# Two layers of cross-attention on one core: values and scores of layer 0 on two 64-row tiles of TensorE

## What is computed

```python
q = x @ Wq + bq;  k = ctx @ Wk + bk;  v = ctx @ Wv + bv
scores = einsum('bkgld,bksd->bkgls', q, k) / sqrt(32) + mask      # 64 keys
out = einsum('bkgls,bksd->bkgld', softmax(scores), v)
x = layer_norm(out @ Wo + bo + x) * gamma + beta
```

## Time and profile before

| what | value |
|---|---|
| median of 3 runs | 1744.62 us (1741.44 to 1746.93) |
| time of the profiled execution | 1741.65 us |
| its span in the profile | 1739.8 us |
| mean granted TensorE clock | 0.999 |
| busy: PE / DVE / POOL / ACT | 98% / 67% / 61% / 33% |

### The profile page before, as it was taken

How to read it: one execution, slowest core, us unless ns; L and a number is a source line. 1 busy time by engine, 2 the same in 40 slices (tenths; PEclk the granted TensorE clock), 3 DMA queues, 4 the chain that set the end, 5 groups by cost and what they waited for, 6 DMA issues and landing times.

```text
span 1739.8 us, 22384 instructions
## 1 busy us (share of the span) xinstructions
PE 1709.9 (98%) x8449; PEld 1426.6 (82%) x8449; DVE 1168.4 (67%) x1106; ACT 581.0 (33%) x669; POOL 1066.3 (61%) x592
## 2 busy tenths in 40 slices
PE   6999999999999999999999999999999999999998
PEld 6888888888888788888888877888888888888887
DVE  7999898888988666565656578446644664466443
ACT  4444354444445433333434223122312231223110
POOL 1777877878788866575756553446734673467331
PEclk9999999999999999999999999999999999999999
DMA  8443244333236577777776856455545654565332
GB/s 239 104 111 86 77 110 108 78 80 78 74 96 165 180 241 228 229 230 224 240 221 223 263 177 194 170 169 182 172 154 170 186 167 155 170 172 180 132 109 97
DMA packets 278127, 280.11 MB, mean 161 GB/s; under 512 B 62330, under 2 KB 230404, under 8 KB 278020
## 3 DMA queue, kind: packets, MB, share of 16 engines
q1 hardware_dynamic: 276672, 276.97, 52.4%
q10 hardware_dynamic: 1348, 1.71, 0.3%
HBM read 175.81 MB, written 102.76 MB: 160 GB/s over the span
## 4 chain that ended last, share of the span: by engine, by line
PE 66%; DVE 13%; POOL 10%; issue 5%; ACT 4%; DMA 2%; SPq 0%; POOLq 0%; DVEq 0%; ACTq 0%
PE ps L53 21%; PE ps L54 21%; PE ps L55 21%; POOL pT0l L1382 3%; POOL pr L1386 2%; DVE small L1106 1%; PE ps L712 1%; PE ps L720 1%; DVE pT1r L1137 1%; DVE pT0r L1137 1%; DVE pr L1126 1%; ACT pT1h L880 1%; ACT pr L852 1%; DVE xT0r L1039 1%; POOL xb L1408 1%
## 5 line engine op out<-in xcount | busy, mean ns | idle before, releaser
L1459 POOL TENSOR_TENSOR x2Tl<-x2r,x2Th 128x1024 fp32r<-128x1024 f32 x31 | 74.5, 2403 | 274.6 <-ACT x2Th L972 274.6
L1236 DVE STREAM_TRANSPOSE x2r<-xd 128x1024 f32<-128x1024 f32 x32 | 68.8, 2148 | 199.9 <-PE ps L55 199.9
L1391 POOL TENSOR_TENSOR pr<-pr,small 128x1024 f32<-128x1024 f32 x64 | 121.9, 1905 | 95.0 <-DVE small L1132 94.9
L972 ACT CAST x2Th<-x2r 128x1024 fp32r<-128x1024 f32 x32 | 33.6, 1051 | 366.9 <-DVE x2r L1236 366.9
L1386 POOL TENSOR_TENSOR pr<-pr,small 128x1024 f32<-128x1024 f32 x64 | 121.9, 1905 | 8.4 <-DVE small L1110 6.0
L1408 POOL TENSOR_TENSOR xb<-xb,bo 128x1024 f32<-128x1024 f32 x32 | 76.9, 2403 | 72.6 <-DMA xb<-in_x_dram 72.6
L1106 DVE TENSOR_REDUCE small<-pr 128x16 f32<-128x1024 f32 x64 | 78.1, 1220 | 45.6 <-ACT pr L852 45.6
L1422 POOL TENSOR_TENSOR y<-y,bet 128x1024 f32<-128x1024 f32 x31 | 74.4, 2400 | 55.7 <-DVE y L1154 55.7
L1154 DVE TENSOR_TENSOR y<-y,gam 128x1024 f32<-128x1024 f32 x32 | 56.1, 1752 | 70.9 <-ACT y L893 70.9
L53 PE MATMUL ps<-wo0h,oc0l 128*128 128x512 f32 x256 | 102.3, 399 | 0.0
L53 PE MATMUL ps<-wo0h,oc1l 128*128 128x512 f32 x256 | 101.6, 397 | 0.4 <-DVE y L1191 0.4
(11 more groups left out here) (379 smaller groups left out, 5442.4 us busy)
## 6 DMA issues: line engine op xcount, KB each, us to landing
xr<-in_x_dram SPq DMA_DIRECT2D x128, 128.0 KB, 2.9
o_scratch<-ot SPq DMA_DIRECT2D x256, 64.0 KB, 1.8
ocr<-o_scratch SPq DMA_DIRECT2D x16, 1024.0 KB, 8.6
xb<-in_x_dram SPq DMA_DIRECT2D x32, 512.0 KB, 6.9
a_scratch<-ost SPq DMA_DIRECT2D x64, 256.0 KB, 3.5
b_scratch<-ost SPq DMA_DIRECT2D x64, 256.0 KB, 5.9
xd<-x_scratch SPq DMA_DIRECT2D x128, 128.0 KB, 2.9
raw<-b_scratch SPq DMA_DIRECT2D x64, 256.0 KB, 5.7
```

Of the source, the lines that this page charges most:

```text
L1236: nc.vector.transpose(x2r[:].rearrange("p k (t j) -> p t k j", t=TPB), xd[:].rearrange("p t (i k) -> p t k i", k=KT)).then_inc(x2_turned, 1)
L1391: nc.gpsimd.tensor_tensor(heads(v), heads(v), mx.unsqueeze(2).to_broadcast([P, TPB * GRP, KEYS]), ALU.subtract)\
L1459: nc.gpsimd.tensor_tensor(x2T[1][:], x2r[:], f32(x2T[0][:]), ALU.subtract).then_inc(x2_lo, 1)
```

## The change

- **Values.** The high and low parts of V stand side by side in the columns of the stationary operand (`vb` is now 64 rows by 2 parts by 2 heads by 32). Each of the two 64-row tiles (`h`) handles two heads and all 512 columns, and writes its own PSUM bank. Four pairs of 64-row matmuls take the place of six 128-row ones. Rows 0 to 63 of the result hold the high part's share, rows 64 to 127 the low part's. ACT evicts 128x1024 instead of 128x512.
- **The sum of the two shares** is made by a transfer that POOL issues, 64 rows of 1024 onto 64 others with an addition (`accum_op`). SP waits for it (`o_sum`) before it stores, a slot later than before.
- **Scores.** Each of the 12 matmuls of 128 rows and 256 columns becomes a pair of 64 rows and 128 columns, two heads in each.
- **Buffers.** Values use both PSUM banks of a unit, so they wait for the eviction of unit v-1. `qs` has one buffer, since `ot` (now 4 KB each) takes the place of the other.
- **Order.** PE now runs query steps 0 to 5, values, scores, query steps 6 and 7. The `chunk0` pieces go from POOL to DVE's next slot, and so does one low part of the probabilities, that of unit 62.

```diff
+def summed_in(u):
+    if 5 <= u < UNITS + 3:
+        return [u - 5] if u < UNITS + 2 else [u - 5, u - 4]
+    return [u - 4] if u == UNITS + 3 else []
...
-        vb = [at(f"vb{i}", 164 + 2 * i, [P, 2, 2, P], F32R) for i in range(2)]
+        vb = [at(f"vb{i}", 164 + 2 * i, [P, 2, 2, 2, HD0], F32R) for i in range(2)]
...
-                if 4 <= u < UNITS + 4:
-                    v = u - 4
-                    sp.wait_ge(o_ev, v + 1)
+                for v in summed_in(u):
+                    sp.wait_ge(o_sum[v % 2], 16 * (v // 2 + 1))
...
-                    after(pe, o_ev, v - 1)
-                    for c in range(2):
-                        last = three(nc, V[v % 2], [vb[v % 2][:, c, x] for x in (0, 1)], [pT[v % 2][x][:, c].rearrange("p j n -> p (j n)") for x in (0, 1)],
-                                     c == 0, c == 1)
+                    after(pe, o_ev, v)
+                    for n, (c, x) in enumerate(((0, 1), (0, 0), (1, 1), (1, 0))):
+                        for h in range(2):
+                            rows = slice(64 * h, 64 * (h + 1))
+                            last = nc.tensor.matmul(V[h], vb[v % 2][rows, c].rearrange("p x a d -> p (x a d)"),
+                                                    pT[v % 2][x][rows, c].rearrange("p j n -> p (j n)"), start=n == 0, stop=n == 3)
...
-                    query(range(0, 4))
+                    query(range(0, 6))
                 if 4 <= u < UNITS + 4:
                     values_of(u - 4)
-                if u < UNITS:
-                    query(range(4, 6))
...
-                        last = three(nc, S[v % 2][:, 256 * m:256 * (m + 1)], [qs[v % 2][x][:, m] for x in (0, 1)],
-                                     [kb[v % 2][:, :, x] for x in (0, 1)], True, True)
+                        for n, (x, y) in enumerate(((1, 0), (0, 1), (0, 0))):
+                            for r in range(2):
+                                rows = slice(64 * r, 64 * (r + 1))
+                                last = nc.tensor.matmul(S[v % 2].rearrange("p (j m s) -> p j m s", j=GRP, m=TPB)[:, 2 * r:2 * r + 2, m], qs[x][rows, m],
+                                                        kb[v % 2][rows, 2 * r:2 * r + 2, y], start=n == 0, stop=n == 2)
...
-                    nc.scalar.copy(ot[v % 2][:].rearrange("p (j i m) -> p j i m", j=GRP, m=TPB),
-                                   V[v % 2].rearrange("p (j m i) -> p j i m", j=GRP, m=TPB)).then_inc(o_ev, 1)
+                    nc.scalar.copy(ot[v % 2][:].rearrange("p h (j i m) -> p (h j) i m", j=GRP, m=TPB),
+                                   VV.rearrange("p (j m i) -> p j i m", j=2 * GRP, m=TPB)).then_inc(o_ev, 1)
...
-                    after(act, scores, u - 1)
-                    nc.scalar.activation(qs[u % 2][0][:], Q[u % 2].rearrange("p (n m) -> p m n", m=TPB), ACT.Identity,
+                    after(act, scores, u)
+                    nc.scalar.activation(qs[0][:], Q[u % 2].rearrange("p (n m) -> p m n", m=TPB), ACT.Identity,
...
+                if (i := chunk0(u - 1)) is not None:
+                    dve.wait_ge(oc_hi, i + 1)
+                    nc.vector.tensor_tensor(oT[0][1][:, 2 * i:2 * i + 2], oc[0][:, 2 * i:2 * i + 2],
+                                            f32(oT[0][0][:, 2 * i:2 * i + 2]), ALU.subtract).then_inc(oc_lo, 1)
+                if u == UNITS:
+                    v = UNITS - 2
+                    dve.wait_ge(p_hi, v + 1)
+                    nc.vector.tensor_tensor(pT[v % 2][1][:], pTr[v % 2][:], f32(pT[v % 2][0][:]), ALU.subtract).then_inc(p_lo, 1)
...
-                if 3 <= u < UNITS + 3:
+                for v in summed_in(u):
+                    pool.wait_ge(o_ev, v + 1)
+                    nc.gpsimd.dma_start(ot[v % 2][:64], ot[v % 2][64:], accum_op=ALU.add).then_inc(o_sum[v % 2], 16)
+                if 3 <= u < UNITS + 3 and u != UNITS + 1:
```

More of the change, by code:

```diff
@@ L101, in program @@
         kf, vf = at("kf", 202, [P, 2, CTX]), at("vf", 204, [P, 2, KV0])
-        qs = [[at(f"qs{i}{x}", 152 + 4 * i + 2 * j, [P, TPB, P], F32R) for j, x in enumerate("hl")] for i in range(2)]
+        qs = [at(f"qs{x}", 152 + 2 * j, [P, TPB, P], F32R) for j, x in enumerate("hl")]
         kb = [at(f"kb{i}", 160 + 2 * i, [P, GRP, 2, KEYS], F32R) for i in range(2)]
-        vb = [at(f"vb{i}", 164 + 2 * i, [P, 2, 2, P], F32R) for i in range(2)]
+        vb = [at(f"vb{i}", 164 + 2 * i, [P, 2, 2, 2, HD0], F32R) for i in range(2)]
         pr = [at(f"pr{i}", 168 + 4 * i, [P, GRP, TPB, KEYS]) for i in range(2)]
@@ L109, in program @@
               for i in range(2)]
-        ot = [at(f"ot{i}", 202 + 2 * i, [P, BLK]) for i in range(2)]
+        ot = [at(f"ot{i}", o, [P, 2, BLK]) for i, o in enumerate((202, 156))]
         mask = [at(f"mask{i}", 192 + i, [P, TPB, KEYS]) for i in range(2)]
@@ L171, in program @@
         V = [ps[:, 3072 + HALF * i:][:, :HALF] for i in range(2)]
+        VV = ps[:, 3072:4096]
         C2 = ps[:, 0:2048]
@@ L184, in program @@
         w_ld, x_ld, k_ld, v_ld, o_st = sems("w_ld", 4), sems("x_ld", 4), sems("k_ld", 2), sems("v_ld", 2), sems("o_st", 2)
+        o_sum = sems("o_sum", 2)
         (wo_hi, wo_lo, c_ld, oc_hi, oc_lo, o_done, xbo, y_done, st_done, aggr, coef, applied, scaled, normed,
@@ L1125, in slot @@
                     dve.wait_ge(scores, v + 1)
-                    nc.vector.tensor_tensor(p[:].rearrange("p j m s -> p m j s"),
-                                            S[v % 2].rearrange("p (m j s) -> p m j s", m=TPB, j=GRP),
-                                            mask[t % 2][:].unsqueeze(2).to_broadcast([P, TPB, GRP, KEYS]), ALU.add)\
+                    nc.vector.tensor_tensor(p[:].rearrange("p j m s -> p j (m s)"),
+                                            S[v % 2].rearrange("p (j c) -> p j c", j=GRP),
+                                            mask[t % 2][:].rearrange("p m s -> p (m s)").unsqueeze(1).to_broadcast([P, GRP, TPB * KEYS]), ALU.add)\
                         .then_inc(s_read, 1)
@@ L1140, in slot @@
                     dve.wait_ge(q_hi, u + 1)
-                    nc.vector.scalar_tensor_tensor(out=qs[u % 2][1][:], in0=Q[u % 2].rearrange("p (n m) -> p m n", m=TPB), scalar=bq[:, u % KT:u % KT + 1],
-                                                   in1=f32(qs[u % 2][0][:]), op0=ALU.add, op1=ALU.subtract).then_inc(q_lo, 1)
+                    nc.vector.scalar_tensor_tensor(out=qs[1][:], in0=Q[u % 2].rearrange("p (n m) -> p m n", m=TPB), scalar=bq[:, u % KT:u % KT + 1],
+                                                   in1=f32(qs[0][:]), op0=ALU.add, op1=ALU.subtract).then_inc(q_lo, 1)
                 for g in wq_late(u):
@@ L1166, in split_wt @@
                 def split_wt(f, i):
+                    if f == 0 and i == 0:
+                        dve.wait_ge(o_st[1], 64 * UNITS // 2)
                     dve.wait_ge(wT_hi, 2 * f + i + 1)
@@ L1392, in slot @@
                         .then_inc(centered, 1)
-                if (i := chunk0(u)) is not None:
-                    chunk_lo(0, i, 2)
                 if u - 2 * KT in (3, 4, 5):
```

10 lines of the change are left out of this document (5 added, 5 removed).

## The result

The changed kernel takes 1752.94 us (median of 6 runs, 1750.00 to 1754.57), the kernel before 1743.95 in the 6 runs beside them. The ratio is 1.0049 with a 95% interval of 1.0038 to 1.0059: about 8.5 us slower. The forecast was 1745, within a range of 1735 to 1769. So the range held and the forecast itself did not: it said no measurable change, and there is one. (The medians themselves are 9.0 us apart; the 8.5 is the ratio's.)

A forecast was written before the change was run, and what follows sets the result against it. PE was taken to set the pace, with a DVE, ACT and POOL loop 0.07 us per slot pair behind. 1741.65 + 4.3 - 3.4 - 1.1 + 0.9 = 1742.4 us, in medians 1745; range 1735 to 1769.

The forecast's parts named there:

- value pair, score pair: PE's attention matmuls on 64-row tiles: a values pair every 0.226 us, a scores pair every 0.113.
- PE's slot: PE's work per attention slot: 0.45 + 0.07 saved, 0.38 lost changing tiles, so 0.14 us shorter, to 8.13.
- freed from PE, attention and last slots: Attention gains 3.4 us from PE's pace and moved chunk0 pieces; slots 56 to 63, without x tiles, gain 1.1.
- issue on POOL: Issuing the sum's transfer takes POOL 1.0 us, delaying the low part 0.16 us per pair of slots: +4.3 us.
- stores and evictions: Attention slots: ACT's doubled eviction and SP's store a slot later were taken to cost nothing.
- seam: End of attention: POOL issues two transfers ahead of unit 63's low part, making PE late: +0.9 us.
- The loop: DVE, ACT and POOL cycle in attention, 16.47 us per two slots before; 16.6 expected after, limiting PE's gain.
- rival 3: DVE's subtraction in attention also holds POOL's transfer issue, delaying the low part: +31 us, 1772; chance 0.12.
- What I cost at nothing: Attention: larger eviction, single qs, values waiting for the previous eviction, later stores, transfer landing, mask addition; all taken as 0.
- The first: Attention: transfer issue hidden, loop closes up behind faster PE, 0.14 us off all 64 slots; 1734 us; chance 0.20.
- The second's price: POOL's transfer issue in attention is long, 1.85 us: +27 us, giving 1768; chance 0.22.
- the fourth's: Attention pairs run one after the other, over 2 us a slot, +130 us; with late evictions or waiting stores, chance 0.06.

The follow-up runs named there:

- no sum: Changed kernel without the accumulating transfer, so the two shares of the values are not added; timed 1738.96 us, ratio 0.9972 to the kernel before.
- stores first: Changed kernel with SP's attention stores issued right behind the keys, ahead of x tile, values and mask; 1747.52 us, ratio 1.0017 to the kernel before.
- two issues: Changed kernel with each unit's sum sent as two transfers of 64x512 instead of one; 1764.79 us, ratio 1.0120 to the kernel before.
- mended kernel: Changed kernel with earlier attention stores, Wk1 and Wv1 loads behind unit 59's store, Wq1 and Wo1 before unit 63's, POOL's last sums later; 1742.69 us, ratio 0.9994.
- weight loads behind: Changed kernel with SP's loads of layer 1's Wk and Wv moved behind the store of unit 59; 1751.63 us, ratio 1.0042 to the kernel before.

## Why the prediction was right or wrong

| step | forecast | measured |
|---|---|---|
| value pair, score pair | 0.226, 0.113 us | 0.23, 0.11 |
| PE's slot | 8.13 us | 8.06 to 8.10 |
| freed from PE, attention and last slots | -4.5 us | -3.9 and -5.9 (no sum) |
| issue on POOL | +4.3 us | 0.9 in one pair of slots, else about 0 |
| stores and evictions | 0 | +4.0 (stores first) |
| seam | +0.9 us | +7.0, and 1.7 in the rest |

- **PE and its tiles: right.** The steps in and out of the tiles, the weight-load pace of the scores and the pairs of the values together came out within 0.07 us of a slot. The Trainium skill's speedup of up to 2x for 64-row operands (TensorEngine Tiling (Array Packing), Theoretical Speedup) is not seen for these scores: a pair took 0.112 us where a full matmul took 0.119, and with them alone, the slot grew.
- **The loop: right in kind.** It was the bound, at 16.48 us and not at the forecast 16.6; a slot of PE that is 0.17 to 0.21 us shorter gave the attention stage 4 to 6 us, not 10 to 13, once nothing else was in the way.
- **The issue: mis-sized.** I took 1.0 us on POOL, of which 0.16 a pair would show. It measured 0.84 recorded, and rival 3 is ruled out: the issue started beside DVE's subtraction and was not held (123.06 lies in 122.84 to 124.20), and the low part behind it ended 2.25 us behind DVE as before. The Trainium skill says that DVE's operations with two SBUF inputs block only those operations of POOL that read SBUF (SBUF — State Buffer, SBUF: two separate sides). This trace agrees. The lower end that I gave, nothing, was the right one for one issue, but for the one pair in which POOL had nothing to spare.
- **What I cost at nothing: wrong, and this is the first step that failed.** "SP stores a slot later; behind its wait stand the loads of keys and values" looked only at who stands behind the store. I did not ask what stands ahead of it, nor who waits for it: ACT's next eviction into the same `ot`, and through it PE, since the values now wait for the last eviction and not the one before. Here the stores cost 4.0 us, which the mis-sized issue happened to balance. That the attention stage, forecast at -0.2, came out at -0.3 is luck.
- **The seam: wrong, and this is where the result lies.** "POOL now issues two transfers" counted their length and left out what each waits for. The second waits for unit 62's eviction, that one for PE, PE for the eviction of unit 61, and that for a store behind 7.8 us of weight loads. The last transfer, which leaves at 598.95, holds SP until 602.37, and with it the next residual tile. I forecast 0.9 us there and found 7.0. Each chain mended alone brought 0.1 (SP's) and 1.4 us (POOL's); the last store moved on top of the first brought 2.6; the two chains together, with the earlier stores and the loads of Wq1 and Wo1 moved up, 3.4. How much of this is PE's lower clock and how much the order is open.
- **The signs.** By the signs that I gave, the pairs came as described. The distance of 16.48 and the low part's start 0.53 us behind the subtraction of the maximum (1.1 was given) spoke for the first rival, and "if PE waits for evictions" came to pass. PE's waits for the low part of the query came in ten slots between 60 and 560 us, not in most pairs, though its weight loads waited for it 30 times (17.3 us in all); its busy share stayed at 98%.
- **Rivals.** The first (1734) came closest in mechanism, with the issue hidden; without the sum's costs the kernel is at 1739. Its loop didn't give way. The second's price (1768) is about that of two issues (1764.8). The range, said to start at the first rival, starts 1 us above it. What did happen was in the fourth's "a store that waits", at 0.06 with others.

What stays open: the mended kernel is 2.3 us longer at the seam than the one without the sum, and I didn't separate POOL's three issues there from the last store's landing. No two kernels differ in PE's clock at the seam and in nothing else, so its share of the 7.0 us, up to 3.4, isn't known. The 1.7 us in the rest of the span, of which 1.1 lie behind the thirteenth addition, weren't traced.

## What to carry to other kernels

When a transfer is put between an eviction and a store, list for that buffer everything that stands ahead of the store in its queue and everyone who waits for it, and do this once for the steady loop and once for each place where the loop ends. A cost that hides behind another engine's operation is free only up to that cover: the first issue cost nothing but in the one pair where POOL was full, a second one 0.6 to 0.7 us a pair. And mending the longest wait alone can bring nothing: after the edit, look where the idle time went and what the clock did, before calling the wait harmless.

## What the runs showed of the hardware

- A transfer issued by POOL with an addition, 64 rows of 4 KB within SBUF, occupied POOL for 0.84 us as recorded (median; 0.81 to 1.01) and landed in 3.7 us (median). POOL's operation right behind it was recorded as starting 0.25 us before the issue's end and as longer by about as much (2.40 alone, 2.65 to 2.70 behind an issue), so 0.84 is about what it takes from POOL.
- Twelve score matmuls of 128 rows and 256 columns and twelve pairs of 64 rows and 128 columns take nearly the same time: 0.119 against 0.112 us each, and 0.2 a slot more for the steps in and out of the tiles.
- SP took 1.9 to 2.6 us to issue four transfers in most places, but 5.61 and 5.92 for the four right behind a load of 1 MB at the seam (the weights in the changed kernel, `vb` with the weight loads behind), and 3.78 there before.
- PE's granted clock fell to its lower level, 1.2 of 2.4 GHz, in or just behind idle times of PE of 5.25 and 2.30 us (for 6.9 and 3.4 us, changed kernel), 2.03 (for 3.5, before) and 3.79 (for 6.9, weight loads behind). In the mended kernel it stayed at 2.4 GHz with idle times of 2.48 and 2.80. So the length of one idle time doesn't decide it by itself. At the lower level the pairs at 582.66 and 583.09 are 0.43 us apart, not 0.23. The windows of the changed kernel (engines' busy us, then the clock, DMA share, GB/s) show 0.60 and 0.54, where before the same windows had 0.60 and 0.97:

```profile
579.00:583.00 4.00, 0.90 (x4) 0.86 (x6) 1.99 (x3) 1.48 (x2) 3.67 (x2) 0.60 0.53 106
583.00:587.00 4.00, 4.00 (x14) 2.71 (x11) 0.98 (x3) 3.27 (x4) 2.50 (x6) 0.54 0.30 64
```
